# The last stage of a graph transformer layer: block order on VectorE, the place of the weight turn, and two outputs from PSUM

## The reference

```python
x = x + gnn(xn, ...) + mix(xn, ...)          # x1
# ffn(layernorm(x1)), added to x1:
weights = einsum('bsd,do->bso', xn2, wr) + br           # one weight per token
_, idx = top_k(weights, k); sel_idx = idx[:, :kk]       # the kk largest
h = gelu(einsum('bkd,dh->bkh', sel, w1) + b1)           # 256 -> 1024
y = (einsum('bkh,hd->bkd', h, w2) + b2) * w_sel         # 1024 -> 256
out = x1 + (xn2 + y where selected, xn2 elsewhere)
```

## Time and profile before

| | us |
|---|---|
| median of 3 runs | 868.28 |
| span of the profiled execution, first to last instruction | 864.6 |
| TensorE busy | 709.8 (82%) |
| VectorE busy | 596.9 (69%) |
| GpSimd busy | 513.7 (59%) |
| ScalarE busy | 231.3 (27%) |

### The profile page before, as it was taken

One profiled execution on the slowest core, in us unless ns is written; L12 is line 12 of the kernel. 1 busy time (PEld: TensorE's weight loads), 2 busy tenths in 40 slices (PEclk: granted clock), 3 DMA queues, 4 the chain that ended last, 5 costly groups with the idle time before them and its releaser, 6 DMA issues.

```text
span 864.6 us, 18704 instructions
## 1 busy us (share of the span) xinstructions
PE 709.8 (82%) x4369; PEld 541.9 (63%) x4370; DVE 596.9 (69%) x1630; ACT 231.3 (27%) x915; POOL 513.7 (59%) x512
## 2 busy tenths in 40 slices
PE   3799687887878798868787878787876998999995
PEld 2576665555555565545565546465555987999994
DVE  7665277565657576657675757676667991999985
ACT  1133502111212122213132323232333442333331
POOL 5242537777777777778777777777751070333332
PEclk9899799776769776777787868787787998999998
DMA  6254325554556555554555545555420002000000
GB/s 202 69 170 80 95 59 132 128 123 121 123 125 129 125 124 129 121 124 119 122 128 128 128 115 126 126 119 120 115 79 1 1 1 78 19 31 26 32 25 21
DMA packets 104859, 82.97 MB, mean 96 GB/s; under 512 B 67133, under 2 KB 91566, under 8 KB 104561
## 3 DMA queue, kind: packets, MB, share of 16 engines
q0 software_dynamic: 18816, 52.21, 22.6%
q1 hardware_dynamic: 85873, 29.16, 15.6%
HBM read 74.47 MB, written 6.84 MB: 94 GB/s over the span
## 4 chain that ended last, share of the span: by engine, by line
POOL 37%; issue 26%; PE 21%; DVE 9%; DMA 4%; SPq 2%; POOLq 1%; DVEq 0%; ACT 0%; ACTq 0%
POOL G L380 37%; PE ps L561 8%; PE ps L574 7%; PE ps L414 2%; PE ps L420 2%; DVE wprod L1086 1%; DMA x<-in_x 1%; DVE G L1069 1%; DVE x L1073 1%; DVE stats L739 1%; DVE x L1027 1%; DMA dstm_d<-wide 1%; DMA htab<-hst 1%; DVE acc L1079 1%; DMA G<-htab,srcr 1%
## 5 line engine op out<-in xcount | busy, mean ns | idle before, releaser
L380 POOL DMA_INDIRECT G<-htab,srcr x392 | 419.3, 1070 | 149.9 <-issue 138.3
L480 PE MATMUL ps<-msg,oh 128*128 128x260 f32 x784 | 303.0, 525 | 74.0 <-DVE oh L992 73.7
L480 PEld LDWEIGHTS ps<-msg,oh 128*128 128x128 f32 x784 | 176.6, 249 | 105.0 <-issue 78.9
L930 DVE TENSOR_TENSOR msg<-G,msg 128x1024 f32<-128x1024 f32 x98 | 119.8, 1222 | 32.8 <-issue 22.2
L561 PEld LDWEIGHTS ps<-xnT,w 128*128 128x128 f32 x800 | 98.3, 201 | 3.8 <-issue 1.8
L561 PE MATMUL ps<-xnT,w 128*128 128x128 f32 x800 | 98.8, 285 | 2.1 <-ACT wide L721 1.6
L663 ACT ACTIVATE negR<-ps 128x1 f32<-128x1 f32 x98 | 16.8, 171 | 291.2 <-PE ps L476 253.9
L574 PE MATMUL ps<-w,wide 128*128 128x256 f32 x400 | 90.4, 379 | 1.0 <-DVE acc L1093 1.0
L393 POOL TENSOR_SCALAR G<-acc,mw 128x256 f32<-128x256 f32 x25 | 23.1, 926 | 99.6 <-DVE mw L1126 90.4
L449 PE MATMUL ps<-ad,ohT 128*128 x1464 | 74.7, 176 | 8.7 <-issue 4.5
L992 DVE TENSOR_TENSOR oh<-iota,dmr 128x512 f32<-128x512 f32 x98 | 67.4, 687 | 19.8 <-issue 19.0
(11 more groups left out here) (137 smaller groups left out, 801.8 us busy)
## 6 DMA issues: line engine op xcount, KB each, us to landing
dstb<-dstu_d SPq DMA_DIRECT2D x98, 128.0 KB
G<-htab,srcr POOLq DMA_INDIRECT x392
htab<-hst SPq DMA_DIRECT2D x25, 130.0 KB, 3.2
out<-G SPq DMA_DIRECT2D x24, 128.0 KB, 1.7
x<-in_x SPq DMA_DIRECT2D x4, 640.0 KB, 8.0
w<-in_L_ffn_w SPq DMA_DIRECT2D x4, 512.0 KB
kq<-w_d SPq DMA_DIRECT2D x1, 1600.0 KB, 6.3
dmr<-dstm_d SPq DMA_DIRECT2D x98, 2.0 KB
```

The costliest lines, as they stand in the source:

```text
L380: gp.indirect_dma_start(G[:, q % RING, k, :], None, htab, bass.IndirectOffsetOnAxis(ap=srcr[:, q, k:k + 1], axis=0)).then_inc(s_g[q % RING ...
L480: m = pe.matmul(ps[:, 3 + p, 0:ROW], oh[:, p, k, :], msg[:, p, k, :], start=(k == 0), stop=(k == TILES - 1))
L930: dve.tensor_tensor(msg[:, p, :, 0:HF].rearrange("p k (h o) -> p k h o", h=HEADS), G[:, q % RING, :, 0:HF].rearrange("p k (h o) -> p k h o ...
```

## The change

- VectorE works through `add_graph` block by block: multiply, add, statistics, aggregate, each waiting for the one before it. The batches for the square root are blocks 0 and 1, 2 to 7, and 8 to 24 (before: 0, 1 to 4, and 5 to 24).
- ScalarE's square root of blocks 2 to 7 stands behind Gelu(0) and that of blocks 8 to 24 behind Gelu(3). Gelu's table is loaded behind take_tokens(0).
- Within the third batch VectorE puts in weigh and take for blocks 0, 1, 2, behind blocks 14, 19 and 23; in the loop of norms it does take(3), take(4), take(5) behind norms 8, 15 and 22.
- The weights are turned behind down(7) (WT_AT = 8). VectorE waits for their spread ahead of take(8), and the ranks of a step stand ahead of its take.
- For blocks 23 and 24 (DIRECT = 23) GpSimd forms b2 times mw, adds x, and leaves it in x as the base. VectorE does the remaining ranks, and then writes y from PSUM times mw plus the base to `ob` in one instruction (`write_output`). SyncE waits for that one.

```diff
-        FIRST_BATCHES = ((0, 1), (1, BODY - 1))
+        BATCHES = ((0, 2), (2, 8), (8, NB))
-        WT_AT = 6
+        WT_AT = 8
+        DIRECT = NB - 2
...
@@ SyncE
-                    sp.wait_ge(S["out_staged"], t + 1)
+                    if t < DIRECT:
+                        sp.wait_ge(S["out_staged"], t + 1)
+                    else:
+                        sp.wait_ge(S["direct_out"], t - DIRECT + 1)
...
@@ GpSimd
-                gp.wait_ge(S["y_taken"], t + 1)
                 gp.wait_ge(S["xn2_added"], t + 1)
                 gp.wait_ge(S["rank_steps"], 2 * t + 2)
...
+                if t < DIRECT:
+                    gp.wait_ge(S["y_taken"], t + 1)
+                    gp.tensor_scalar(ob[:, t % 4, :], acc[:, t, 0:D], mw[:, t:t + 1], None, ALU.mult).then_inc(S["y_weighted"], 1)
+                else:
+                    gp.tensor_scalar(ob[:, t % 4, :], b2b[:, :], mw[:, t:t + 1], None, ALU.mult).then_inc(S["y_weighted"], 1)
                 gp.wait_ge(S["y_weighted"], t + 1)
+                if t < DIRECT:
+                    gp.tensor_tensor(ob[:, t % 4, :], ob[:, t % 4, :], x[:, t, :], ALU.add).then_inc(S["out_staged"], 1)
+                else:
+                    gp.tensor_tensor(x[:, t, :], ob[:, t % 4, :], x[:, t, :], ALU.add).then_inc(S["output_based"], 1)
...
@@ ScalarE
-            for base, n in FIRST_BATCHES:
-                deviation(base, n, NB + base + n)
-                if base == 0:
-                    take_tokens(0)
+            deviation(0, BATCHES[0][1], NB + BATCHES[0][1])
+            take_tokens(0)
             act.activation(negR[:, 0:1], eps[:, 0:1], ACT.Gelu_apprx_tanh).then_inc(S["gelu_table"], 1)
...
-                if t == BODY - 2:
-                    deviation(BODY, NB - BODY, 2 * NB)
+                for at, (lo, hi) in zip((0, 3), BATCHES[1:]):
+                    if t == at:
+                        deviation(lo, hi - lo, NB + hi)
...
@@ VectorE
+            def add_graph(t):
+
+                r = rden[:, 1, t, :].unsqueeze(2).to_broadcast([P, HEADS, OUT_F])
+                g = gsc[:, t % BODY, :]
+                dve.tensor_tensor(g.rearrange("p (h o) -> p h o", h=HEADS), acc[:, t, 0:HF].rearrange("p (h o) -> p h o", h=HEADS), r, ALU.mult).then_inc(S["x1_steps"], 1)
+                dve.wait_ge(S["x1_steps"], 2 * t + 1)
+                dve.tensor_tensor(x[:, t, :], x[:, t, :], g, ALU.add).then_inc(S["x1_steps"], 1)
+                dve.wait_ge(S["x1_steps"], 2 * t + 2)
+                dve.bn_stats(stats[:, t % BODY, :], x[:, t, :]).then_inc(S["stats_ready"], 1)
+                dve.wait_ge(S["stats_ready"], NB + t + 1)
+                dve.bn_aggr(mv[:, t, :], stats[:, t % BODY, :]).then_inc(S["mean_var_ready"], 1)
...
+            def write_output(t):
+
+                dve.wait_ge(S["y_ready"], t + 1)
+                dve.wait_ge(S["output_based"], t - DIRECT + 1)
+                dve.wait_ge(S["rank_steps"], 2 * t + 2)
+                dve.scalar_tensor_tensor(out=ob[:, t % 4, :], in0=ps[:, 4 + t % 3, 0:D], scalar=mw[:, t:t + 1], in1=x[:, t, :], op0=ALU.mult, op1=ALU.add).then_inc(S["direct_out"], 1)
+
+            for k, (lo, hi) in enumerate(BATCHES[:2]):
+                for t in range(lo, hi):
+                    add_graph(t)
+                invert(lo, hi - lo, NB // BODY + 1 + k)
+                for t in range(lo, hi):
                     norm_tokens(t)
-            for i in range(1, NB // BODY):
-                add_graph(i * BODY, BODY)
-            invert(BODY, NB - BODY, NB // BODY + 1 + len(FIRST_BATCHES))
-            for t in range(BODY, NB):
+            taken = 0
+            lo, hi = BATCHES[2]
+            for t in range(lo, hi):
+                add_graph(t)
+                if t in (lo + 6, lo + 11, lo + 15):
+                    weigh_tokens(taken)
+                    take_output(taken)
+                    taken += 1
+            invert(lo, hi - lo, NB // BODY + 3)
+            weighed = taken
+            for t in range(lo, hi):
                 norm_tokens(t)
-                weigh_tokens(t - BODY)
-                if t % 4 == 3:
-                    take_output(t // 4 - 1)
-            for t in range(NB - BODY, NB):
+                weigh_tokens(weighed)
+                weighed += 1
+                if t in (lo, lo + 7, lo + 14):
+                    take_output(taken)
+                    taken += 1
+            for t in range(weighed, NB):
                 weigh_tokens(t)
-            taken = NB // 4 - 1
...
             for t in range(taken, NB):
-                take_output(t)
-                if t == WT_AT + 1:
+                if t == WT_AT:
                     dve.wait_ge(S["weights_spread"], 16)
-                if t >= WT_AT + 1:
+                if t >= WT_AT:
                     for _ in range(min(1 + t % 2, NB - ranked)):
                         rank_tokens(ranked)
                         ranked += 1
+                if t < DIRECT:
+                    take_output(t)
+                else:
+                    while ranked < NB:
+                        rank_tokens(ranked)
+                        ranked += 1
+                    write_output(t)
```

More of the change, by code:

```diff
@@ L187, in gps_layer @@
                      "weights_turned weights_taken weights_stored weights_spread counted rank_steps xn2_added "
-                     "xn2_ready xn2_turned xn2T_ready hidden_ready gelu_ready y_ready y_taken out_staged "
+                     "xn2_ready output_based direct_out xn2_turned xn2T_ready hidden_ready gelu_ready y_ready y_taken out_staged "
                      "split_steps acc_zeroed").split():
@@ L392, in _ @@
                     gp.wait_ge(s_out[t % 4], 16 * (t // 4))
-                gp.tensor_scalar(ob[:, t % 4, :], acc[:, t, 0:D], mw[:, t:t + 1], None, ALU.mult).then_inc(S["y_weighted"], 1)
+                if t < DIRECT:
[3 more added lines that the diff above has]
+                    gp.tensor_scalar(ob[:, t % 4, :], b2b[:, :], mw[:, t:t + 1], None, ALU.mult).then_inc(S["y_weighted"], 1)
                 gp.wait_ge(S["y_weighted"], t + 1)
-                gp.tensor_tensor(ob[:, t % 4, :], ob[:, t % 4, :], x[:, t, :], ALU.add).then_inc(S["out_staged"], 1)
+                if t < DIRECT:
+                    gp.tensor_tensor(ob[:, t % 4, :], ob[:, t % 4, :], x[:, t, :], ALU.add).then_inc(S["out_staged"], 1)
+                else:
+                    gp.tensor_tensor(x[:, t, :], ob[:, t % 4, :], x[:, t, :], ALU.add).then_inc(S["output_based"], 1)
         @block.tensor
@@ L1093, in take_output @@
                 dve.tensor_tensor(acc[:, t, 0:D], ps[:, 4 + t % 3, 0:D], b2b[:, :], ALU.add).then_inc(S["y_taken"], 1)
[L1095 to L1098, removed]
-                    norm_tokens(t)
-            for i in range(1, NB // BODY):
-                add_graph(i * BODY, BODY)
-            invert(BODY, NB - BODY, NB // BODY + 1 + len(FIRST_BATCHES))
-            for t in range(BODY, NB):
-                norm_tokens(t)
-                weigh_tokens(t - BODY)
-                if t % 4 == 3:
-                    take_output(t // 4 - 1)
-            for t in range(NB - BODY, NB):
+            def write_output(t):
[8 more added lines that the diff above has]
+                for t in range(lo, hi):
+                    norm_tokens(t)
+            taken = 0
[9 more added lines that the diff above has]
+            for t in range(lo, hi):
+                norm_tokens(t)
+                weigh_tokens(weighed)
[4 more added lines that the diff above has]
+            for t in range(weighed, NB):
                 weigh_tokens(t)
-            taken = NB // 4 - 1
             def rank_tokens(t):
```

## The result

The changed kernel takes 871.51 us (median of 20 runs), the kernel before 866.47 us over as many: a ratio of 1.0067 (95% interval 1.0047 to 1.0088). By the ratio that is 5.8 us slower (4.1 to 7.6); the two medians by themselves lie 5.0 us apart. The forecast was 6.7 us slower, from 868.28 to 875.0.

The account below looks back on a forecast made before the run. TensorE was taken to bound the last stage: down(24) ends 5.2 us later and, with ranks and output, the span grows 6.7, from 864.6 to 871.3; plus the median's 3.7 gives 875.0 us, range 871.0 to 878.4.

Parts of the forecast that it names:

- A: The forecast, chance 0.70: ScalarE's wait for block 24 stalls up(5); 875.0 us.
- First batch: Block 1 takes its four steps before the first square root; norm(0), turn(0), up(0) and later TensorE work begin 1.45 us later.
- list of three: TensorE's losses before the change: up(1) waits 1.60 us for a Gelu, down(3) 1.01 for a take, up(7) 4.04 for a weigh.
- Second batch: Blocks 2 to 7: norm(2) at 672.8 us, turn(2) due at 673.6 just doesn't wait; two added table loads cost nothing.
- Third batch: Blocks 8 to 24, VectorE: block 24 aggregated at 704.8 us, including 2.6 for GpSimd's additions, 2.7 for weigh and take pairs.
- The stall: Behind Gelu(3) ScalarE waits 13 us instead of 0.25; up(5) stands 9.2 us and loses 2.83 more to the clock.
- The ranks: On VectorE, they start 8.35 us behind the turn of the weights, at 748.5, cost 4.19 each; rank(24) ends about 861.7.
- The tail: End of the span: direct output follows rank(24) and GpSimd's two steps, at 864.4 us against 857.7 before, +6.7.
- B: Rival, chance 0.08: waiting for one's own previous step costs VectorE nothing over a batch; up(5) stalls 3.9 us; 869.7 us.
- C: Rival, chance 0.04: B, and GpSimd's additions cost 0 instead of 2.6 us; up(5) waits 1.3 us; 864.3 us.
- D: Rival, chance 0.06: the ranks keep up and the output follows down(24) directly; 870.8 us.
- E: Rival, chance 0.12: GpSimd's additions cost twice as much, or turn(2) misses norm(2), 2.6 us more; 877.6 us.

Follow-up runs that it names:

- experiment 5: The kernel before with only the weights' turn moved behind down(7), spread awaited at block 8, ranks ahead of the take; ratio 0.9938, stage 195.6 us.
- experiment 8: The kernel before with the turn behind down(7), ranks ahead of the take, two ranks ahead of even takes; ratio 0.9949, stage 193.9 us.
- experiment 4: The changed kernel with two ranks ahead of even takes and one ahead of odd ones, instead of one and two; ratio 1.0040, stage 203.4 us.
- experiment 2: The changed kernel with add_graph in batches again (2; 3, 3; 4, 3, 5, 4, 1 blocks); ratio 1.0016, stage 201.1 us.
- experiment 3: The changed kernel without the direct output, last two outputs by take_output and GpSimd as before; ratio 1.0064, stage 206.9 us.

## Why the prediction was right

The mechanism is the one forecast (A), and each step can be read off; times are given from the start of the stage where the two executions differ. The time itself, 871.51 us, lies 3.5 us under the forecast and only 0.5 us above the lower end of its range. 1.8 of the 3.5 us are the chance of the three runs shown: the kernel before has a median of 866.47 over 20 runs, not 868.28. The rest is the difference between the two kernels, and most of that is the first point below.

- *First batch.* turn(0) comes 4.04 us into the stage instead of 2.59: 1.45 later, as worked out. up(1) is only 0.65 later, because up(0) took 5.48 us and not 6.28, as it had in the kernel before:

```profile
659.29 0.69 PE L551 MATMUL ps<-ident,acc 128*128 128x128 f32 x2 [5.53 <-DVE acc L1079]
660.45 6.28 PE L561 MATMUL ps<-xnT,w 128*128 128x128 f32 x32 [0.47 <-ACT xnT L706]
```

That is the term that was mis-sized. up(0) runs in good part at the slow clock (granted 0.50 from 662 to 664 in the kernel before), a loss that the prediction's list of three leaves out. I took its length as fixed; in the ten profiled executions of this study it lies between 5.04 and 6.39 us, in no order with the change. The 0.8 us runs through everything behind it and is nearly the whole gap between +6.7 and +5.9, so in these two executions that part of the gap is chance. It also counts only after the change: in the order before, down(3) waits for a take that doesn't hang on up(0), and starts 38.6 us into the stage with up(0) at 6.28, 6.18 and 5.04 us (before, experiments 5 and 8). In the changed order that wait is gone, and VectorE's third batch follows Gelu(0): with up(0) 0.56 us longer (experiment 4), down(3) starts 0.55 us later.
- *By block.* The steps lie 0.46 us apart and a block costs 1.45 us; experiment 2 shows the price.
- *Second batch.* norm(2) comes 15.3 us into the stage (forecast 16.1, the same 0.8), turn(2) doesn't wait, and Gelu(1) starts at 677.59, 1.6 us ahead of up(2): the added table loads are hidden, though with only 0.3 us to spare over the 1.28 us by which up(1) and up(5) followed the Gelu that they waited for.
- *Third batch.* From norm(2) to the aggregation of block 24: 32.1 us, forecast 32.0. The six norms and the two steps behind them took about 2.4 us more than 0.35 us a norm and 0.46 us a step, while GpSimd did its six additions (forecast 2.6; no run moves the additions away, so that they are the cause is argued); the three pairs of weigh and take cost 0.97 to 1.02 us each (forecast 0.9).
- *The stall.* ScalarE waits 12.8 us (13), up(5) 9.07 us (9.2), and from up(5) to up(6) are 10.03 us (10.07). The drain that the Trainium skill ("ScalarE: Activation LUTs", section "What ACT_TABLE_LOAD costs") puts behind a table load isn't there: the load at 707.54 ends at 708.82 and Gelu(4) starts at 708.84.
- *The turn of the weights* doesn't wait and costs 0.11 us (0.15).
- *The ranks* start 8.33 us behind the turn (8.35) after a wait of 7.7 us on VectorE; from there to the first direct output are 113.5 us (113.2). They begin here:

```profile
750.21 3.46 DVE L1146 TENSOR_SCALAR_CACHE_REDUCE kq<-kq,wtok 128x3125 f32<-128x3125 f32 x1 [7.70 <-issue]
```

- *The tail* is 4.9 us behind down(24) (4.8), and experiments 3 and 4 show that the ranks, not the direct output, decide it.

The rivals: B and C fall with experiment 2, D with experiments 3 and 4 (even with 2.7 us gained the output doesn't follow down(24)), E with the 32.1 us and with turn(2), which didn't wait.

## What to carry to other kernels

A batch that one engine finishes as a whole and a second engine waits for has its price at the place of that wait in the second engine's list: the same late work cost 9 us of TensorE, and the clock behind it, when ScalarE waited two blocks too soon, and 1.8 us, at the turn of the weights, when the wait stood two blocks later. When work is reordered, read off when the last of a batch is done and move the waits for it with it. On VectorE, steps that wait for their own predecessor cost 0.46 us here and the same steps in batches 0.36, which is worth keeping where the engine is on the path; and an output made one step shorter is worth nothing while something else, here the ranks, arrives last.

## What the runs showed of the hardware that was not expected

The length of the slow stretch behind a wait isn't fixed by the wait. After 9.07, 9.07 and 9.06 us of waiting up(5) took 6.51, 6.47 and 5.18 us; after 4.47 us it took 5.44, and up(7) of the kernel before, after 4.04 us, 6.56. An up at 2.4 GHz, granted clock 1.00, takes 3.73. The granted clock tells the same, first the changed kernel (up(5) from 710.12), then experiment 4 (from 710.66):

```profile
713.00:715.00 2.00, 2.00 (x12) 2.00 (x11) 2.00 (x7) 0.00 (x0) 1.56 (x2) 0.50 0.00 0
```

```profile
712.00:714.00 2.00, 2.00 (x13) 2.00 (x12) 2.00 (x7) 0.00 (x0) 1.62 (x2) 0.61 0.00 0
714.00:716.00 2.00, 2.00 (x20) 2.00 (x19) 2.00 (x7) 0.00 (x0) 1.54 (x3) 1.00 0.00 0
```

Waits of 1.78, 1.80 and 1.84 us left the next up or down within 0.07 us of its short time. So a wait of several microseconds cost 1.4 to 2.8 us more in these executions, and a charge of 2.83 for it, as in the prediction, is its upper end.
